# A graph-attention layer: the bias of the target side as a 33rd row of the edge weights, and a longer run of first gathers

## The reference, cut to what matters

```python
h  = relu(layernorm(x))
xm = h @ W_n2m.T                      # (N, 128)
ea = edge_attr @ W_r2m.T              # (E, 128)
xl = xm @ Wl.T + bl                   # source side
xr = xm @ Wr.T + br                   # target side
loop_attr = segment_mean(ea, dst)     # attributes of each node's own loop edge
e  = concat(ea, loop_attr) @ We.T
u  = leaky_relu(xl[src] + xr[dst] + e, 0.2)
logits = einsum("ehd,hd->eh", heads(u), att)
alpha  = softmax of logits over the edges of one dst
out    = segment_sum(heads(xl)[src] * alpha, dst) + bias
return x + out @ W_m2n.T
```

## Time and profile before

| | us |
|---|---|
| median of 3 runs | 2258.5 |
| lowest and highest run | 2256.99 and 2272.94 |
| the profiled execution | 2253.14 |
| span of that execution, first to last instruction | 2251.4 |

### The profile page before, as it was taken

One profiled execution on the slowest core, in us unless ns is written; L12 is line 12 of the kernel. 1 busy time (PEld: TensorE's weight loads), 2 busy tenths in 40 slices (PEclk: granted clock), 3 DMA queues, 4 the chain that ended last, 5 costly groups with the idle time before them and its releaser, 6 DMA issues. The chain is left out here.

```text
span 2251.4 us, 61984 instructions
## 1 busy us (share of the span) xinstructions
PE 2144.1 (95%) x11913; PEld 1376.3 (61%) x11914; DVE 1472.7 (65%) x4241; ACT 1543.6 (69%) x4420; POOL 1595.4 (71%) x1693
## 2 busy tenths in 40 slices
PE   8898999999999999999999999999999999999977
PEld 7645666556665666566656665666666656666655
DVE  7535666666666766676666675666666666666686
ACT  6335777767776777677767776777677767777753
POOL 6477777777777777777777777777777777777203
PEclk9978999999999999999999999999999999999999
DMA  6244444445445544454445444444454545444237
GB/s 231 65 117 108 120 122 118 113 118 122 119 111 120 123 118 116 116 124 119 111 118 124 119 115 115 124 118 112 117 125 120 116 114 125 117 116 115 63 83 115
DMA packets 309959, 263.62 MB, mean 117 GB/s; under 512 B 172165, under 2 KB 281290, under 8 KB 308780
## 3 DMA queue, kind: packets, MB, share of 16 engines
q1 hardware_dynamic: 251570, 145.37, 24.5%
q0 software_dynamic: 57632, 113.02, 22.0%
q10 hardware_dynamic: 346, 0.82, 0.1%
HBM read 247.57 MB, written 16.89 MB: 117 GB/s over the span
## 5 line engine op out<-in xcount | busy, mean ns | idle before, releaser
L782 POOL DMA_INDIRECT xl_g<-xl_table,src_tab x1612 | 1532.9, 951 | 514.9 <-issue 473.2
L1001 PE MATMUL banks<-msg,onehot 128*128 128x177 f32 x3416 | 646.8, 333 | 4.5 <-ACT msg L1056 4.0
L1001 PEld LDWEIGHTS banks<-msg,onehot 128*128 128x128 f32 x3416 | 530.9, 194 | 169.4 <-issue 140.8
L1147 DVE SCALAR_TENSOR_TENSOR uT<-banks,uT 128x512 f32<-128x512 f32 x427 | 295.1, 691 | 505.9 <-ACT uT L1063 499.6
L1025 ACT ACTIVATE xl_z<-xl_g 128x256 f32 x854 | 308.9, 408 | 363.8 <-DMA xl_g<-xl_table,src_tab 315.8
L1047 ACT ACTIVATE distance<-iota_n,minus_slot 128x128 f32<-128x128 f32 x1708 | 539.2, 386 | 0.0
L956 PE MATMUL banks<-attrT,Wc 32*128 32x512 f32 x854 | 490.2, 654 | 0.0
L952 PE MATMUL banks<-onehotT,xr_parts 128*128 128x256 bf16 x2562 | 361.2, 278 | 29.8 <-issue 20.6
L960 PEld LDWEIGHTS banks<-ident,xl_z 128*128 128x128 f32 x1708 | 182.1, 142 | 332.8 <-issue 280.5
L1125 DVE TENSOR_TENSOR msg<-xl_g,banks 128x256 f32<-128x256 f32 x854 | 319.4, 415 | 79.4 <-PE banks L1001 63.4
L1063 ACT ACTIVATE uT<-banks 128x512 f32<-128x512 f32 x427 | 250.4, 587 | 120.3 <-PE banks L960 119.1
(11 more groups left out here) (191 smaller groups left out, 1342.9 us busy)
## 6 DMA issues: line engine op xcount, KB each, us to landing
slot_bc<-slot_dram SPq DMA_DIRECT2D x427, 128.0 KB
attrT<-in_attr_cols SPq DMA_DIRECT2D x854, 32.0 KB
rbf<-in_attr_rows SPq DMA_DIRECT2D x854, 32.0 KB
xl_g<-xl_table,src_tab POOLq DMA_INDIRECT x1612
masks<-masks_dram SPq DMA_DIRECT2D x108, 96.5 KB
out<-in_x SPq DMA_DIRECT2D x16, 336.0 KB
out<-xl_g POOLq DMA_DIRECT2D x6, 896.0 KB, 8.7
xl_g<-xl_table SPq DMA_DIRECT2D x7, 448.0 KB, 6.6
```

The costliest lines, as they stand in the source:

```text
L782: pool.indirect_dma_start(out=xl_g[:, g % PRING, i], out_offset=None, in_=xl_table, in_offset=bass.IndirectOffsetOnAxis(ap=src_tab[:, j:j ...
L1001: mm = nc.tensor.matmul(U_ps[j % 2][:, h], onehot[:, j % 2, t], msg[:, j % 2, t], start=i == 0, stop=i == PT - 1)
L1147: nc.vector.scalar_tensor_tensor(out=uT[:, s % URING], in0=z_ps[s % 2], scalar=SLOPE, in1=uT[:, s % URING], op0=ALU.mult, op1=ALU.add).the ...
```

## The change

`br` leaves the xr stage. It becomes the 33rd row of the weights that edge attributes are multiplied with (`Wc_br`), and `attrT` gets a 33rd row of ones, set once. The finale, whose mean attributes are multiplied with `Wc` as before, gets `br` by a one-row matmul of its own for each half batch. The x rows move from places 13 to 61 of the ring to places 15 to 63; the head takes 17 pieces (34 gathers); those of places 0 to 14 wait for no group of the xr stage, and those of places 15 and 16 for the group that holds the x rows in their places (the first). The wait for `w_copied`, and the set-up count, grow by one each. Functions get the new tiles as arguments; those lines are left out here.

```diff
-HEAD_PIECES = 13
+X_AT = PRING - WINDOWS
+HEAD_PIECES = 17
...
+        Wc_br = sb("Wc_br", [D_RBF + 1, D_MSG])
+        rows_in_w = sb("rows_in_w", [1, (1 + GW + 1) * D_MSG])
+        br_rows = rows_in_w[:, D_MSG:(1 + GW) * D_MSG]
...
-        x_sb = xl_g[:, HEAD_PIECES:HEAD_PIECES + WINDOWS].rearrange("p w i d -> p w (i d)")
+        x_sb = xl_g[:, X_AT:X_AT + WINDOWS].rearrange("p w i d -> p w (i d)")
...
             for j in range(HEAD_GATHERS):
-                if j % PT == 0 and j:
-                    pool.wait_ge(xr_done, j // PT)
+                if j % PT == 0 and j // PT >= X_AT:
+                    pool.wait_ge(xr_done, (j // PT - X_AT) // GW + 1)
                 gather(pool, xl_g, xl_table, src_tab, landings, landed, j)
...
             act.dma_start(last_weights[:], out_weights).then_inc(last_weights_in, 16)
+            act.dma_start(Wc_br[D_RBF:D_RBF + 1, :], weight_rows[:, D_MSG:2 * D_MSG]).then_inc(br_in, 16)
...
             nc.scalar.activation(att_bc[:], wps[1][:, D_MSG:2 * D_MSG], ACT.Copy).then_inc(w_copied, 1)
+            nc.scalar.activation(Wc_br[0:D_RBF, :], wps[1][0:D_RBF, 0:D_MSG], ACT.Copy).then_inc(w_copied, 1)
+            act.wait_ge(br_in, 16)
             for p, ws in enumerate(pairs):
...
                 for w in ws:
-                    n = w % GW
-                    project(xr_ps[g % 4][:, n], w, 1)
-                    mm = nc.tensor.matmul(xr_ps[g % 4][:, n], ones[0:1, :], br_rows[:, n * D_MSG:(n + 1) * D_MSG],
-                                          start=False, stop=True)
+                    mm = project(xr_ps[g % 4][:, w % GW], w, 1)
                 mm.then_inc(xr_done, 1)
...
-        attrT = sb("attrT", [D_RBF, TRING, GROUP])
+        attrT = sb("attrT", [D_RBF + 1, TRING, GROUP])
...
-        SET_UP, ACC_PARTS = 4, 7
+        SET_UP, ACC_PARTS = 5, 7
...
-                        sp.dma_start(attrT[:, s % TRING, h * PIECE:(h + 1) * PIECE],
+                        sp.dma_start(attrT[0:D_RBF, s % TRING, h * PIECE:(h + 1) * PIECE],
...
-                    nc.tensor.matmul(z, Wc[0:D_RBF], attrT[:, s % TRING], start=False, stop=False)
+                    nc.tensor.matmul(z, Wc_br[:], attrT[:, s % TRING], start=False, stop=False)
...
             nc.vector.memset(msg[:, :, :, MSG:CNT], 1.0).then_inc(set_up, 1)
+            nc.vector.memset(attrT[D_RBF:D_RBF + 1], 1.0).then_inc(set_up, 1)
...
                 for lo, hi in halves:
+                    nc.tensor.matmul(z_ps[:, lo:hi], ones[0:1, :], br_rows[:, 0:(hi - lo) * D_MSG], start=True, stop=False)
                     for part in range(PARTS):
                         nc.tensor.matmul(z_ps[:, lo:hi], ident16[:], xr_parts[:, n * FB + lo:n * FB + hi, part],
-                                         start=part == 0, stop=False)
+                                         start=False, stop=False)
```

More of the change, by code:

```diff
@@ L182, in gat_kernel @@
                  (x_cols, src_cols, dst_rows, dst_lasts, first_weights, out_weights, weight_rows),
-                 xr_parts, ident, ident16, ones, iota_n, node_of, att_bc, att_pad, Wc, last_weights,
+                 xr_parts, ident, ident16, ones, iota_n, node_of, att_bc, att_pad, Wc, Wc_br, rows_in_w, last_weights,
                  minus_slot, src_tab, tabs, piece_tab, walk_tab, step_tab, sums_tab, free_tab, xl_g, landings, landed)
@@ L187, in gat_kernel @@
         edge_loop(nc, banks, xl_table, slot_dram, masks_dram, attr_rows, attr_cols,
-                  xr_parts, ident, ident16, ones, iota_n, node_of, att_pad, Wc, minus_slot, src_tab, walk_tab,
+                  xr_parts, ident, ident16, ones, iota_n, node_of, att_pad, Wc_br, minus_slot, src_tab, walk_tab,
                   step_tab, sums_tab, piece_tab, free_tab, xl_g, landings, landed, acc, x, out)
-        finale(nc, banks, x, xl_table, xr_parts, ident, ident16, att_bc, Wc, W_outT, bias_col, xl_g, acc, out)
+        finale(nc, banks, x, xl_table, xr_parts, ident, ident16, ones, br_rows, att_bc, Wc, W_outT, bias_col, xl_g, acc, out)
 def prologue(nc, banks, xl_table, slot_dram, masks_dram, inputs,
-             xr_parts, ident, ident16, ones, iota_n, node_of, att_bc, att_pad, Wc, last_weights,
+             xr_parts, ident, ident16, ones, iota_n, node_of, att_bc, att_pad, Wc, Wc_br, rows_in_w, last_weights,
              minus_slot, src_tab, tabs, piece_tab, walk_tab, step_tab, sums_tab, free_tab,
@@ L240, in prologue @@
         Wall = sb("Wall", [P, 4, D_MSG])
-        rows_in_w = sb("rows_in_w", [1, (1 + GW + 1) * D_MSG])
         bn = sb("bn", [P, WINDOWS, 6])
@@ L252, in prologue @@
                            W_in[:, D_NODE + 3 * D_MSG:])
-        bl_row, br_rows, att_row = (rows_in_w[:, 0:D_MSG], rows_in_w[:, D_MSG:(1 + GW) * D_MSG],
-                                    rows_in_w[:, (1 + GW) * D_MSG:])
+        bl_row, att_row = rows_in_w[:, 0:D_MSG], rows_in_w[:, (1 + GW) * D_MSG:]
         att_col = last_weights[:, D_NODE + 1:D_NODE + 2]
@@ L260, in prologue @@
         xl_out = [sem(f"xl_out{i}") for i in range(LRING)]
-        weights_in, weight_rows_in, last_weights_in, lasts_in = map(
-            sem, ("weights_in", "weight_rows_in", "last_weights_in", "lasts_in"))
+        weights_in, weight_rows_in, br_in, last_weights_in, lasts_in = map(
+            sem, ("weights_in", "weight_rows_in", "br_in", "last_weights_in", "lasts_in"))
         rows_in = [sem(f"rows_in{i}") for i in range(CHUNKS)]
@@ L532, in walk_sums @@
                 pe.wait_ge(met_ready, 1)
-                pe.wait_ge(w_copied, 4)
+                pe.wait_ge(w_copied, 5)
                 nc.tensor.matmul(free_ps, ones16[:], met[:], start=True, stop=True).then_inc(met_counted, 1)
@@ L551, in project @@
                 nc.tensor.matmul(to, x_sb[:, w, 0:P], Wall[:, of], start=True, stop=False)
-                return nc.tensor.matmul(to, x_sb[:, w, P:2 * P], Wall[:, 2 + of], start=False, stop=of == 0)
+                return nc.tensor.matmul(to, x_sb[:, w, P:2 * P], Wall[:, 2 + of], start=False, stop=True)
             pe.wait_ge(ident_ready, 1)
@@ L787, in edge_loop @@
 def edge_loop(nc, banks, xl_table, slot_dram, masks_dram, attr_rows, attr_cols,
-              xr_parts, ident, ident16, ones, iota_n, node_of, att_pad, Wc, minus_slot, src_tab, walk_tab, step_tab, sums_tab,
+              xr_parts, ident, ident16, ones, iota_n, node_of, att_pad, Wc_br, minus_slot, src_tab, walk_tab, step_tab, sums_tab,
               piece_tab, free_tab, xl_g, landings, landed, acc, x, out):
@@ L1207, in _, with finale @@
                                             ).then_inc(rescaled, 1)
-def finale(nc, banks, x, xl_table, xr_parts, ident, ident16, att_bc, Wc, W_outT, bias_col, xl_g, acc, out):
+def finale(nc, banks, x, xl_table, xr_parts, ident, ident16, ones, br_rows, att_bc, Wc, W_outT, bias_col, xl_g, acc, out):
     with ExitStack() as ctx:
```

## The result

The changed kernel takes 2254.8 us (median of 19 runs, 2248.9 to 2260.9); the kernel before, in 19 runs beside it, 2274.4. The ratio, taken over all runs and not from the two medians, is 0.9934, with a 95% interval of 0.9911 to 0.9958: the changed kernel is faster by 0.7%, within 1% as forecast, and close to the forecast ratio (2247.5 / 2258.5 = 0.9951). That agreement hides an error, because the times of the kernel before fall in two groups, and this difference can't be understood without them: over all 81 runs beside this study's kernels, 36 lie at 2252.0 to 2260.7 (mean 2255.9) and 45 at 2272.9 to 2283.8 (mean 2277.3). The changed kernel has one group. So two things happened.

The account below looks back on a forecast made before the run. The prediction took GpSimd's gathers as the bound, TensorE close behind. Gathers ending earlier -19.1, small additions +0.2 and finale +8.0 sum to -10.9 us from 2258.5, about 2247.5 us; range 2235 to 2259.

Parts of the forecast that it names:

- likeliest case: Whole kernel: 6 to 15 us faster, range 2243 to 2253 us, chance 0.62.
- the 1.94 us of before: Prologue's end: time from the mask stores' landing to the loop's first gather, assumed unchanged after the 34th gather's end.
- The bound: Loop: GpSimd's gathers stay the bound; TensorE, some 52 us behind, keeps 42 us of starved time.
- The xr stage and the head: Prologue: windows of 0.44 us, stage done near 85 us, 34th gather at 98.6, loop's first gather at 102.0.
- The sum of 19.1: End of the gathers: loop's gathers start 9.1 us earlier and 8 fewer gathers save 10.0 us, together 19.1 us.
- The 33rd row: Loop matmul L956: 33 rows for 32 cost 0 us; a loss up to 0.10 us a step would be hidden.
- the rival of 2290.6 us: Loop matmul L956: one more height change adds 85 us, 42 hidden, and TensorE becomes the bound; chance 0.05.
- The small additions: Prologue and loop set-up: ScalarE copy 0.2 us, br's load hidden, one-row memset about 1.4 us counted as 0.
- The finale: Finale's one-row matmuls: 2.3 us a batch, 16 us in all, 5.9 hidden for certain, 3.3 perhaps; 8.0 us taken.
- The rival with a hidden finale: Finale: one-row matmuls fit beside VectorE's work and give nothing back, 2239.6 us; chance 0.16.
- The rival that the head gives less: Prologue: gathers stretch beside VectorE work or the stage ends late, so only the 8 gathers are gained, 2256.7 us; chance 0.17.

Follow-up runs that it names:

- The head alone: The kernel before with a head of 34 unpaced gathers, br staying in the xr stage: ratio 0.9934, seven runs at mean 2245.7 us, five at 2266.8.

## Why the prediction was right or wrong

*The time.* 2254.8 us were measured and 2247.5 forecast; 2254.8 lies outside the range of 2243 to 2253 that the prediction gave its likeliest case. The mechanism held in the main (the stage gets short, GpSimd stays the bound, the finale pays), but what ends the block was not, as the prediction had it, the 1.94 us of before, and other terms of the sum were mis-sized too: in the two profiles the change gives 3.7 us and not 10.9. Of the 7.2 us that are missing, 3.1 are the end of the block, 2.8 the gather step, 0.8 the finale and 0.7 the stretch before it; the first gather gives 0.2 back. That the ratio agrees (0.9934 for 0.9951) is luck: it comes from the upper group, which the prediction did not know.

*The bound.* Right. GpSimd has no wait above its 0.3 us step in the loop, TensorE did not become the bound, and every kernel's end follows its last gather.

*The xr stage and the head.* Right up to the block's end: 0.44 us a window, VectorE done at 82.8 us for 85, the 34th gather at 98.81 for 98.6. The sentence that failed is "With the 1.94 us that the block end and the loop's start took before, the loop's first gather would start at 101.5". The 1.94 us were measured from the mask stores' landing, but with the stores out of the way it is GpSimd's own drain that ends the block, 3.5 us after its last gather, and the gap is 5.29 us. So the loop's first gather starts at 105.05 us where 102.0 was forecast, and the lower bound of 101.5 could not be reached; that the drain ended at the same time as SP stood in the trace of the kernel before. This is 3.1 us of the missing 7.2.

*The sum of 19.1 and whom it belongs to.* I gave 10.0 us to the 34 gathers. The head alone does earn them, 10.2 us, but only while the xr stage is long. With the short stage they are worth nothing (2250.4 with 26 paced gathers, 2250.7 with 34). The count should have been of GpSimd's idle time between its first gather and the loop: 111.09 - 57.19 - 26 x 1.256 = 21.2 us before, 105.05 - 56.86 - 34 x 1.256 = 5.5 us after. By that the last gather comes 16 us earlier; 13.3 were seen in this pair of profiles, since the gather step came out as 1.2575 us for 1.2557, 2.8 us in 1577 steps. Over the 13 profiles of this study the step runs from 1.254 to 1.258 with no order by kernel, so I take that for scatter between executions. It goes with the gathers' own records: the median gather is 944 or 945 ns in the seven profiles with a step of 1.254 to 1.256 us and 947 in the six with 1.257 to 1.258. Why is open.

*The 33rd row.* Right: 854 records at a mean of 654 ns in both kernels, and the rival of 2290.6 us falls. The Trainium skill (TensorE: Matmul & The Clock Gate, Why this matters for your kernels) has a single matmul of 32 rows take the time of one of 128; for 33 against 32 rows the trace shows no difference either.

*The small additions.* The first gather came 0.3 us earlier, not 0.2 later, so the ScalarE copy and the load of br cost nothing that shows. The memset took 1.34 us for 1.4, and no gather waited for it.

*The finale.* Nearly right, 8.8 us for 8.0, but in part by luck. The pairs cost 2.10 us a batch by the period and not 2.3, as the slot of 1.06 us holds a pair with its changes of height. Seven batches of that are 14.7 us, and 14.7 - 8.8 = 5.9 us are hidden, the very sum that the prediction took as certain, but not where it looked for it: the wait before the third batch shrank only from 2.07 to 1.2 us and that before the first transposes from 3.54 to 1.5, the late idle time from 3.3 to 0.3, and the fall of the clock in the first batch, which the prediction did not have, costs some of it again. The rival with a hidden finale falls; its argument, that the chain before ran through VectorE, did not hold for a stage where TensorE was nearly as full: VectorE now waits for TensorE in all seven batches.

*The rival that the head gives less* (2256.7) had the wrong reason: the gathers beside the xr stage's VectorE work hardly stretch (the 34 take 1.271 us each, start to start; the 33 steps are longer by 0.5 us in all, 0.36 of it in one gather of 1.31 us). The Trainium skill (GPSIMD Engine Reference, Key points) names instructions of VectorE in a two-port mode or with two inputs in SBUF as those that contend. The stage's subtractions are not such a case, since one of their two inputs lies in a bank of TensorE's results and not in SBUF, so they are no test of it. The memsets of 128 x 1239 early in the loop have no input at all, and whether they run in a two-port mode no row shows; beside each of them a gather takes 1.3 to 1.9 us (1.80 above, 1.73 in the earlier trace rows).

*The base.* The prediction set its sum against 2258.5, the median of three runs at 2257.0, 2258.5 and 2272.9, and said nothing of the third. It was a run of the upper group. What the change does to the measured ratio is mostly to remove that group: 45 of 81 runs at 21 us make 11.9 us of the mean, more than the 2 to 5 us against the lower one. Nothing in the single profile showed it, but a run 0.6% above the others, of a program with a long stretch of TensorE work on the path, was worth a sentence.

*What stays open.* The upper group was profiled in the head-alone kernel and not in the kernel before. That both have the same cause rests on the same xr stage, the same 21 us and the same lower mean clock. Why the clock falls in about half of the executions is open as well. The rows show only that TensorE had been busy nearly without a pause since 20 us and was in the stage with one-row pairs; the kernels with a short stage end it at 77 to 89 us, and none of their 78 runs lies in an upper group. Whether the length or the one-row pairs matter wasn't tried apart in this stage; in the kernel that adds br there at full height TensorE also pauses ahead of the stage (busy for 3.8 of the 10 us from 50). The falls in the finale speak for the pairs, but in the lower group the same pairs run through the whole xr stage at 1.00.

## What to carry to other kernels

Where an engine with a gap-free stream of work bounds a kernel, count its idle time from its first instruction to its last, and not what is ahead or behind a barrier; and where a barrier ends a stage, list when each engine reaches it, because removing the last one brings only the next one, here 0.0 us behind. A bias added by one-row fp32 matmuls cost 0.62 us for each window of 128 columns in the xr stage and 1.06 us for 512 columns in the finale; as three bf16 parts, spread over rows of the data and picked by one full-height weight tile, 896 columns cost 0.37 us, and the move of the bias became unnecessary. Look at the single times before taking a median: two groups mean that some stretch on the path has two speeds.

## What the runs showed of the hardware

GpSimd's drain at the end of the prologue's block ends 2.9 to 3.6 us after its last gather's record (4.1 in the head alone), and the next gather starts 4.7 to 5.3 us after that record; with SP ending the block it is 1.7 us after SP. TensorE can fall from 2.4 to 1.2 GHz in the midst of a stretch in which it is busy all the time, and stay there: in the profile of the upper group the granted clock is 0.50 in every window from 80 to 160 us, for the first 40 of them with TensorE busy throughout. Where the finale has one-row fp32 pairs, it falls so in each of four profiles, for some 6 us. I had looked for such a fall only where it idles, as in the changed kernel, which has no work for it between 77 and 108 us and 0.50 from 80 to 130 us.
